# Second cross attention of a small perceiver: probabilities turned on VectorE in 32x32 blocks, values of two heads in one product with a ones column

## The chip, the cores and the metric

The kernel runs on one core of one Trainium2 chip. The metric is the device time of one execution in microseconds (us), the median of several. A profile is of one such execution; its times are counted from the first instruction of the span.

## What is computed

Six layers work on x, 64 sequences of 32 tokens with 256 features: a windowed cross attention, an attention, an fp8 feed-forward layer, a second cross attention (the one that is changed), a gated mixing layer and a mixture of experts. Each adds its output to x. The second cross attention, cut to its core:

```python
q = split(layernorm(x) @ w_q + b_q)            # 64 x 16 heads x 32 x 16
k = split(ctx_1024 @ w_k + b_k)                # 64 x 16 heads x 257 x 16
v = split(ctx_1024 @ w_v + b_v)
s = (q @ k.T) * 16 ** -0.5                     # 32 x 257 per head, masked
o = merge(softmax(s) @ v) @ w_o + b_o
x = x + o
```

All of it is float32, and 257 keys are one more than two blocks of 128 and one more than eight blocks of 32.

## The kernel before, in words

x lies in SBUF as 16 tiles `t` of 128 rows; a tile holds 4 sequences `b`. The stage of the second cross attention is `x1_tensor`, `x1_scalar`, `x1_vector` and `x1_pool`, one program for each engine, which meet through counting semaphores. Each goes over 16 tiles and the 4 sequences in each: 64 rounds. TensorE's program is written out for all tiles; the others loop.

Partitions carry (4 strips `j`) x (32 queries), and a round has 4 score groups `rg`, so 16 heads are 4 strips x 4 groups. One round of TensorE before is, in its order:

1. `scores` (L890): 8 products, weights of 32x64 (the spread queries), 257 moving columns, into PSUM banks 2 to 5.
2. second half of `values` of the round before (L918): weights are 32 columns of turned probabilities, moving data 16 columns of values, output in bank 7.
3. pieces `k0` and `k1` of the next sequence (L827): keys from the context, each product as three fp32r products of high and low parts (`exact`). `x1_piece` and `PIECES` write out the order; the pieces alternate between banks 0 and 1, and each needs its bank emptied (`kv0_free`, `kv1_free`).
4. `turn(t, b, 0)` (L903): 4 transposes of probabilities into bank 6.
5. piece `v` of the next sequence (L827), 12 products, 512 columns of one bank.
6. `turn(t, b, 1)` (L903), then the first half of `values` (L918).

In round b = 0 of a tile there is also the 257th key of the tile before: its probabilities are turned (piece `plT`, L865) and multiplied with values of that key made ahead of the stage (`x1_last_values`, `last_rows`, `last_key`, L929). In round b = 1 there is the piece `out` (L869), the output product of the tile before.

VectorE in a round: 4 reductions L1020 (mask, running minimum, `x1_nmax`), the two key copies L1005, the two copies of turned probabilities L1051; once a tile the reciprocals of the sums (L1026 to L1029), the scaling L1035, the block transpose of the heads L1054, the addition to x L1044 and its statistics L1058. ScalarE: 4 exponentials L987 with the sum accumulated, the value copy L972, the split of the next context and the mask. GpSimd: the low part of the context (L1076), the spread queries (L1085), a bias.

## Time and profile before

| | us |
|---|---|
| median of 3 runs | 1004.77 (1001.87 to 1009.84) |
| the profiled execution | 999.8 |
| its span | 998.0 |
| TensorE busy, share of the span | 91% |
| VectorE busy | 68% |
| ScalarE busy | 47% |
| GpSimd busy | 38% |

The span runs from the first to the last instruction of the profiled execution. Busy shares are averages over stages with different limits.

### The profile page before, as it was taken

The numbers are of one execution on the slowest core, as the hardware profiler recorded it, in microseconds if no ns is written. First come the engines' busy times: TensorE is split into PE (matmuls) and PEld (weight loads), VectorE is DVE, ScalarE is ACT, GpSimd is POOL, SyncE is SP. The second block draws the span as 40 slices with busy tenths as digits, with TensorE's granted clock in tenths as the row PEclk, the third lists the DMA queues.
The fourth block names the chain that finished last, engine by engine and source line by source line (L and its number), as shares of the span: only waits on it lengthen the run. The fifth ranks groups of instructions, "written<-read, shape, count | busy, mean of one in ns | idle before, by whom it ended". The sixth has DMA issues, their size and how long they took to land.

```text
span 998.0 us, 39451 instructions
## 1 busy us (share of the span) xinstructions
PE 906.3 (91%) x16050; PEld 741.3 (74%) x16050; DVE 680.4 (68%) x1765; ACT 465.8 (47%) x1197; POOL 381.5 (38%) x602
## 2 busy tenths in 40 slices
PE   4999889989746889999999999999977898999998
PEld 3777777777523678888888888888745568999976
DVE  5888798878775466666666666667568486555536
ACT  1222223322464645555555555556454434555541
POOL 6222223322396162333332242224047305766640
PEclk9999999999767999999999999999879799999999
DMA  7001400000001011111111111110037101222216
GB/s 254 25 19 56 155 4 4 5 4 4 3 1 48 3 50 51 51 50 54 62 66 65 52 50 51 50 50 3 2 132 307 43 0 59 81 75 77 79 65 237
DMA packets 29904, 60.96 MB, mean 61 GB/s; under 512 B 6000, under 2 KB 22480, under 8 KB 26416
## 3 DMA queue, kind: packets, MB, share of 16 engines
q1 hardware_dynamic: 25136, 48.00, 13.6%
q0 software_dynamic: 3744, 10.23, 3.0%
q8 instruction: 130, 2.13, 0.8%
q10 hardware_dynamic: 864, 0.36, 0.2%
q14 instruction: 30, 0.25, 0.1%
HBM read 49.27 MB, written 9.31 MB: 59 GB/s over the span
## 4 chain that ended last, share of the span: by engine, by line
PE 74%; issue 8%; DVE 7%; ACT 4%; POOL 4%; DMA 1%; DVEq 0%; ACTq 0%; POOLq 0%
PE psum L827 18%; PE psum L1605 7%; PE psum L903 7%; PE psum L261 6%; PE psum L234 4%; PE psum L890 3%; PE psum L1468 3%; PE psum L300 3%; PE psum L291 3%; PE psum L918 3%; PE psum L276 3%; ACT x_p L987 2%; PE psum L742 2%; PE psum L869 2%; PE psum L1488 1%
## 5 line engine op out<-in xcount | busy, mean ns | idle before, releaser
L987 ACT ACTIVATE x_p<-x_s,x_nmax 128x257 f32<-128x257 f32 x256 | 127.4, 500 | 100.0 <-DVE x_nmax L1020 99.9
L1051 DVE COPY x_pT<-psum 128x512 f32<-128x512 f32 x128 | 88.2, 689 | 56.3 <-PE psum L903 54.5
L1020 DVE CUSTOM_DVE_ANT_0 x_s<-psum,x_mask 128x257 f32<-128x257 f32 x256 | 94.3, 423 | 41.8 <-PE psum L890 41.1
L1076 POOL TENSOR_TENSOR x_ctx1l<-x_ctx,x_ctx1h 128x2064 fp32r<-128x2064 f32 x8 | 36.8, 4599 | 145.6 <-ACT x_ctx1h L770 145.6
L903 PE MATMUL psum<-ident,x_p 128*128 128x128 f32 x512 | 80.6, 280 | 5.6 <-ACT x_p L987 1.8
L1076 POOL TENSOR_TENSOR x_ctx0l<-x_ctx,x_ctx0h 128x2064 fp32r<-128x2064 f32 x7 | 32.2, 4599 | 104.1 <-ACT x_ctx0h L770 104.1
L903 PEld LDWEIGHTS psum<-ident,x_p 128*128 128x128 f32 x512 | 58.3, 141 | 17.1 <-ACT x_p L987 15.5
L918 PEld LDWEIGHTS psum<-x_v,x_pT 128*32 128x32 f32 x4096 | 48.3, 113 | 30.1 <-DVE x_pT L1051 18.2
L1708 POOL DMA_INDIRECT moe_outs<-me_out,me_goal x39 | 55.1, 1414 | 40.1 <-DVE me_out L1677 40.1
L1005 DVE TENSOR_SCALAR x_k<-psum,x_bk 128x258 f32<-128x258 f32 x128 | 57.7, 481 | 16.1 <-PE psum L827 16.1
L918 PE MATMUL psum<-x_v,x_pT 128*32 128x16 f32 x4096 | 61.0, 186 | 0.0
L972 ACT ACTIVATE x_v<-psum 128x512 f32<-128x512 f32 x64 | 38.2, 597 | 44.0 <-PE psum L827 44.0
L1699 POOL DMA_INDIRECT me_in<-moe_rows,me_token x39 | 39.7, 1018 | 45.3 <-DVE me_token L1454 33.7
L1677 DVE TENSOR_TENSOR me_out<-psum,me_eb 128x256 f32<-128x256 f32 x39 | 16.6, 425 | 58.0 <-PE psum L827 58.0
L325 ACT ACTIVATE sm_xT<-psum 128x256 f32<-128x256 f32 x32 | 12.3, 384 | 90.5 <-PE psum L224 90.5
L234 PE MATMUL psum<-sm_v,sm_pT 32*32 32x17 f32 x4096 | 42.6, 180 | 9.9 <-issue 6.8
L234 PEld LDWEIGHTS psum<-sm_v,sm_pT 32*32 32x32 f32 x4096 | 38.4, 104 | 17.3 <-issue 13.1
L827 PE MATMUL psum<-me_w2h,me_hTh 128*128 x156 | 47.2, 303 | 1.7 <-DVE me_hTl L1680 1.7
L987 ACT ACTIVATION_READ_ACCUMULATOR x_p<-x_s,x_nmax 128x1 f32 x256 | 47.8, 187 | 0.0
L1632 ACT ACTIVATE me_in<-psum 128x256 f32<-128x256 f32 x39 | 15.0, 385 | 67.8 <-PE psum L1592 67.8
L1645 ACT ACTIVATE me_out<-psum,me_eb 128x128 f32<-128x128 f32 x156 | 44.4, 374 | 1.3 <-PE psum L1605 1.3
L890 PE MATMUL psum<-x_k,x_qs 32*64 32x257 f32 x1024 | 44.6, 404 | 0.0
(293 smaller groups left out, 2744.3 us busy)
## 6 DMA issues: line engine op xcount, KB each, us to landing
x_ctx<-in_ctx SPq DMA_DIRECT2D x16, 1032.0 KB, 4.8
me_w<-in_moe_w SPq DMA_DIRECT2D x8, 1024.0 KB, 11.7
me_got<-moe_outs SPq DMA_DIRECT2D x8, 512.0 KB, 7.5
x_mask<-in_mask SPq DMA_DIRECT2D x16, 128.5 KB, 3.8
x<-in_x SPq DMA_DIRECT2D x4, 512.0 KB, 8.0
sm_cT<-in_ctx SPq DMA_DIRECT2D x16, 128.0 KB, 2.2
moe_rows<-me_xw SPq DMA_DIRECT2D x4, 512.0 KB, 4.9
me_ws<-in_moe_ws SPq DMA_DIRECT2D x1, 1024.0 KB, 4.8
```

What stands on the lines that cost most here:

```text
L234: mm = nc.tensor.matmul(psum[strip(b), O, h * DO:(h + 1) * DO], sm_pT[strip(b), u, h * S:(h + 1) * S], sm_v[strip(b), u, h, :], start=True ...
L261: nc.tensor.matmul(psum[:, QK + t % 2, s * D:(s + 1) * D], (kv if s else sm_xT)[:, u, k, :], c.w_qkv[:, k, s * D:(s + 1) * D], start=(s + ...
L827: mm = nc.tensor.matmul(out, v, w, start=(first and n == 0), stop=(last and n == len(pairs) - 1), **kw)
L890: mm = nc.tensor.matmul(psum[2 * S * m:2 * S * (m + 1), 2 + rg, 0:SK], x1_qs[rows, par, m, b, :], x1_k[rows, b % 2, m, 0:SK], start=True, ...
L903: mm = nc.tensor.transpose(psum[:, 6, (2 * r + k) * P:(2 * r + k + 1) * P], x1_p[:, column(b, CB * c + r), k * P:(k + 1) * P], ident[:])
L918: mm = nc.tensor.matmul(psum[S * j:S * (j + 1), 7, n * DH:(n + 1) * DH], x1_pT[:, c, r, k, j * S:(j + 1) * S], x1_v[:, b % 2, k, (j * G + ...
L987: nc.scalar.activation(x1_p[:, n, :], x1_s[:, rg, :], ACT.Exp, bias=x1_nmax[:, par, n:n + 1], scale=-1.0, accum_out=x1_sum[:, par, n:n + 1 ...
L1005: nc.vector.tensor_scalar(x1_k[:, b % 2, m, :], kv_bank(n)[:, 0:SP], x1_bk[:, m:m + 1], None, ALU.add).then_inc(x1[f"kv{n % 2}_free"], 1)
L1020: nc.vector.tensor_tensor_reduce(out=x1_s[:, rg, :], in0=psum[:, 2 + rg, 0:SK], in1=x1_mask[par][:, b, :], scale=1.0, scalar=-2 * MASKED, ...
L1051: nc.vector.tensor_copy(x1_pT[:, c].rearrange("p r k s -> p (r k s)"), psum[:, 6, :]).then_inc(x1["pT_ready"], 1)
L1076: eng.tensor_tensor(low[:], x1_ctx[:], high[:].bitcast(F32), ALU.subtract).then_inc(x1["ctx_split"], 1)
L1605: mm = nc.tensor.matmul(psum[:, i % 2, m * P:(m + 1) * P], me_up[i % 2][:, k * HID + m * P:k * HID + (m + 1) * P], me_sT[:, i % 2, k, :], ...
```

## The change

- The probabilities are no longer turned by TensorE into PSUM and copied. VectorE turns them in 32x32 blocks, from `x1_p` straight to `x1_pT`, 576 elements a partition and half (`turn` in `x1_vector`). `x1_p` has 288 columns: 257 of keys, one of `void` (the old `x1_void`, not a number where everything is masked) and zeros.
- `values` contracts 32 keys at a time. Weights are a block of turned probabilities of two heads, 32 rows x 64 columns; moving data are the values of both heads and a column of ones, 33 columns. Four strips `j` lie in four row groups of the array, strips 0 and 2 in its first 64 columns, 1 and 3 in its last; they write banks 6 and 7. Keys 257 and 258 (`void`) are a ninth block of 2 rows. That is 2 halves x 9 blocks x 4 strips = 72 products a round, in one go, between the key pieces and the value pieces.
- Of each 64x33 output, each head's rows need only their own 16 columns and the sum. `row_pick` is now 128x2 and selects them: VectorE forms reciprocals, multiplies them by `row_pick` and scales both banks with it (`x1_o2`); GpSimd adds the two halves (`x1_heads`).
- The values are made turned, features on partitions, as two pieces `v0` and `v1` with the same shape as the keys, and VectorE turns them in blocks into `x1_v`. The key copies go to ScalarE, whose own value copy goes. ScalarE's exponentials no longer accumulate.
- The output piece `out` becomes `o0` and `o1` of 128 columns each.
- The products, copies, splits, the load and the arrays of the 257th key alone go (`x1_last_values`, `x1_last_scalar`, `last_rows`, `last_key`, `plT`).
- The first value pieces are made after the last query products, and not before them.

The diff without most of the removed lines, which stand in the kernel above:

```diff
@@ -778,12 +744,14 @@
-        PIECES = [("plT", 0, -1), ("k0", 1, 0), ("k1", 1, 0), ("v", 1, 0),
-                  ("k0", 2, 0), ("k1", 2, 0), ("v", 2, 0), ("out", 0, -1),
-                  ("k0", 3, 0), ("k1", 3, 0), ("v", 3, 0),
-                  ("k0", 0, 1), ("k1", 0, 1), ("v", 0, 1)]
-        LEAD = 11
+        PIECES = [("k0", 1, 0), ("k1", 1, 0), ("v0", 1, 0), ("v1", 1, 0),
+                  ("k0", 2, 0), ("k1", 2, 0), ("v0", 2, 0), ("v1", 2, 0), ("o0", 0, -1), ("o1", 0, -1),
+                  ("k0", 3, 0), ("k1", 3, 0), ("v0", 3, 0), ("v1", 3, 0),
+                  ("k0", 0, 1), ("k1", 0, 1), ("v0", 0, 1), ("v1", 0, 1)]
+        LEAD = 14
         CB = BT // 2
+        KB = SK // S + 1
+        VO = 2 * DH + 1
         def column(b, rg):
...
@@ -832,44 +800,33 @@
         def x1_first_pieces(pe):
             pe.wait_ge(x1["w_split"], 4)
...
+            for k in range(2):
                 pe.sem_inc(x1[f"kv{k}_free"], 1)
...
+            for n in (LEAD, LEAD + 1):
                 x1_piece(pe, n, -1, 1, True)
         def x1_piece(pe, n, t, par, there):
             kind, b, whose = PIECES[n]
             kv_free(pe, n, t)
...
+            if not there:
                 pe.sem_inc(x1[f"kv{n % 2}_done"], 1)
                 pe.sem_inc(x1[f"kv{n % 2}_free"], 1)
                 return
...
             out = kv_bank(n)
+            m = slice(int(kind[1]) * P, int(kind[1]) * P + P)
             if kind == "k0" and b == 0:
                 pe.wait_ge(x1["ctx_split"], t + 1 + 1)
...
+            if kind[0] in "kv":
+                ct = x1_cs[(par + 1) % 2 if whose == 1 else par]
                 for k in range(KC):
...
+                    mm = exact(out[:, 0:SP], parts([w[:, k, m] for w in (x1_wks if kind[0] == "k" else x1_wvs)],
+                                                   [c[:, k, b * SP:(b + 1) * SP] for c in ct]), k == 0, k == KC - 1)
+            else:
+                pe.wait_ge(x1["oT_ready"], t)
                 for k in range(KC):
...
+                    mm = nc.tensor.matmul(out[:, 0:P], x1_oT[:, k * P:(k + 1) * P], x1_wo[:, k, m],
                                           start=(k == 0), stop=(k == KC - 1))
             mm.then_inc(x1[f"kv{n % 2}_done"], 1)
...
+            def values(t, b):
+                i = BT * t + b
+                for m in range(KC):
+                    kv_taken(pe, place(f"v{m}", b), t - (b == 0))
+                if i == 0:
+                    pe.wait_ge(x1["ones_ready"], 2)
+                if b == 0 and t > 0:
+                    pe.wait_ge(x1["heads_ready"], 2 * t)
+                for c in range(2):
+                    pe.wait_ge(x1["pT_ready"], 2 * i + c + 1)
+                    for kb in range(KB):
                         for j in range(L):
...
+                            rows = slice(S * j, S * j + (S if kb < KB - 1 else 2))
+                            e = c * BT + b
+                            mm = nc.tensor.matmul(psum[2 * S * (j % 2):2 * S * (j % 2 + 1), 6 + j // 2, e * VO:(e + 1) * VO],
+                                                  x1_pT[rows, b % 2, c, kb, :], x1_v[rows, b % 2, c, kb, :],
+                                                  start=(b + c + kb == 0), stop=False, skip_group_check=True)
                 mm.then_inc(x1["pv_done"], 1)
             def tile(t, par, before, own, after):
                 for b in range(BT):
+                    here = own if b < BT - 1 else after
                     if own:
                         scores(t, par, b)
...
+                    for n in (place("k0", (b + 1) % BT), place("k1", (b + 1) % BT)):
+                        piece(n, t, par, here)
+                    if b > 0 and own or b == 0 and before:
+                        values(t - (b == 0), (b - 1) % BT)
+                    for n in (place("v0", (b + 1) % BT), place("v1", (b + 1) % BT)):
+                        piece(n, t, par, here)
                     if b == 1:
...
+                        piece(place("o0"), t, par, before)
+                        piece(place("o1"), t, par, before)
+            for n in (LEAD + 2, LEAD + 3):
+                piece(n, -1, 1, True)
...
@@ -966,46 +896,57 @@
         def x1_scalar(act):
             nc.scalar.preload_act_table(ACT.Exp)
...
+            def take_keys(b, t, m):
+                n = place(f"k{m}", b)
                 kv_done(act, n, t)
...
+                nc.scalar.activation(x1_k[:, b % 2, m, :], kv_bank(n)[:, 0:SP], ACT.Identity,
+                                     bias=x1_bk[:, m:m + 1]).then_inc(x1[f"kv{n % 2}_free"], 1)
+            for m in range(KC):
+                take_keys(0, -1, m)
             def tile(t, par, before, own, after):
                 for b in range(BT):
...
+                    for m in range(KC):
+                        if own:
+                            for rg in range(CB * m, CB * (m + 1)):
+                                n = column(b, rg)
+                                act.wait_ge(x1["max_ready"], J * t + G * b + rg + 1)
+                                nc.scalar.activation(x1_p[:, n, 0:SK], x1_s[:, rg, :], ACT.Exp, bias=x1_nmax[:, par, n:n + 1],
+                                                     scale=-1.0).then_inc(x1["exp_ready"], 1)
+                        if own if b < BT - 1 else after:
+                            take_keys((b + 1) % BT, t, m)
                     if not after and own and b == 2:
                         mix_normalise(act, 0)
                     if after and b in (0, 1):
                         context_high(act, t + 1, 1 - par, b)
                     if after and b == 2:
                         mask(act, t + 1, 1 - par)
...
             x1_tiles(act, tile)
         def x1_vector(dve):
...
+            def take_values(b, t, i):
+                if not (isinstance(i, int) and i < 2):
+                    dve.wait_ge(x1["pv_done"], i - 1)
                 for m in range(KC):
...
+                    n = place(f"v{m}", b)
                     kv_done(dve, n, t)
...
+                    nc.vector.transpose(x1_v[:, b % 2, m, :, 0:2 * DH], kv_bank(n)[:, 0:KB * S]).then_inc(x1[f"kv{n % 2}_free"], 1)
+            def turn(t, b, c):
+                i = BT * t + b
+                n = column(b, CB * c)
+                hold(dve, x1["exp_ready"], J * t + G * b + CB * (c + 1))
+                if c == 0:
+                    dve.wait_ge(x1["void_ready"], i + 1)
+                if not (isinstance(i, int) and i < 2):
+                    dve.wait_ge(x1["pv_done"], i - 1)
+                nc.vector.transpose(x1_pT[:, b % 2, c].rearrange("p k (r q) -> p r k q", r=CB),
+                                    x1_p[:, n:n + CB, :].rearrange("p r (k s) -> p r k s", s=S)).then_inc(x1["pT_ready"], 1)
+            nc.vector.memset(x1_v[:, :, :, :, 2 * DH:VO].rearrange("p b c k o -> p (b c k o)"), 1.0).then_inc(x1["ones_ready"], 1)
+            take_values(0, -1, 0)
             def tile(t, par, before, own, after):
...
                             nc.vector.tensor_tensor_reduce(out=x1_s[:, rg, :], in0=psum[:, 2 + rg, 0:SK], in1=x1_mask[par][:, b, :], scale=1.0,
                                                            scalar=-2 * MASKED, op0=ALU.add, op1=ALU.min,
                                                            accum_out=x1_nmax[:, par, n:n + 1]).then_inc(x1["max_ready"], 1)
+                        dve.wait_ge(x1["max_ready"], J * t + G * (b + 1))
+                        if isinstance(t, int) and t + b == 0:
+                            dve.wait_ge(x1["ends_ready"], 1)
+                        own_columns = lambda v: v.rearrange("p (c b r) -> p c b r", c=2, b=BT)[:, :, b, :]
+                        nc.vector.tensor_scalar(own_columns(x1_p[:, :, SK]), own_columns(x1_nmax[:, par, :]), 1e10, 0.0, ALU.mult,
+                                                ALU.mult).then_inc(x1["void_ready"], 1)
+                    if b == 1 and before:
+                        dve.wait_ge(x1["o_ready"], t)
+                        nc.vector.transpose(x1_oT[:], x1_o[:]).then_inc(x1["oT_ready"], 1)
+                    if own:
+                        turn(t, b, 0)
                     if b == 0 and before:
...
+                        dve.wait_ge(x1["pv_done"], BT * t)
+                        both = psum[:, 6:8, 0:2 * BT * VO].rearrange("p j (n e) -> p j n e", e=VO)
+                        nc.vector.reciprocal(x1_rinv[:].rearrange("p (j n) -> p j n", j=2), both[:, :, :, 2 * DH]).then_inc(x1["rinv_ready"], 1)
                         dve.wait_ge(x1["rinv_ready"], 2 * t - 1)
...
+                        nc.vector.tensor_tensor(x1_pick[:], x1_rinv[:].unsqueeze(2).broadcast_to([P, 2 * 2 * BT, 2]),
+                                                row_pick[:].unsqueeze(1).broadcast_to([P, 2 * 2 * BT, 2]), ALU.mult).then_inc(x1["rinv_ready"], 1)
+                        dve.wait_ge(x1["rinv_ready"], 2 * t)
+                        if not (isinstance(t, int) and t == 1):
+                            dve.wait_ge(x1["o_ready"], t - 1)
+                        for j in range(2):
+                            own_pick = x1_pick[:, 2 * BT * j:2 * BT * (j + 1), :].unsqueeze(3).broadcast_to([P, 2 * BT, 2, DH])
+                            nc.vector.tensor_tensor(x1_o2[:, :, :, j * DH:(j + 1) * DH], both[:, j, :, 0:2 * DH].rearrange("p n (r d) -> p n r d", r=2),
+                                                    own_pick, ALU.mult).then_inc(x1["heads_ready"], 1)
+                    if own:
+                        turn(t, b, 1)
                     if own if b < BT - 1 else after:
...
+                        take_values((b + 1) % BT, t, BT * t + b + 1)
+                    if b == 1 and before:
+                        hold(dve, x1["x_biased"], t)
+                        for m in range(KC):
+                            n = place(f"o{m}")
                             kv_done(dve, n, t)
...
+                            row = x[:, bass.ds(t - 1, 1), m * P:(m + 1) * P].rearrange("p o c -> p (o c)")
+                            nc.vector.tensor_tensor(row, kv_bank(n)[:, 0:P], row, ALU.add).then_inc(x1[f"kv{n % 2}_free"], 1)
                     if b == BT - 1 and before:
...
+                        for m in range(KC):
+                            n = place(f"o{m}")
+                            hold(dve, x1[f"kv{n % 2}_free"], kv_count(n, t) + 1)
                         nc.vector.bn_stats(bn_out[:, bass.ds(t - 1, 1), :].rearrange("p o c -> p (o c)"),
                                            x[:, bass.ds(t - 1, 1), :].rearrange("p o c -> p (o c)")).then_inc(x1["stats_ready"], 1)
...
+        def x1_heads(pool, t):
+            pool.wait_ge(x1["heads_ready"], 2 * t)
+            if not (isinstance(t, int) and t == 1):
+                pool.wait_ge(x1["oT_ready"], t - 1)
+            nc.gpsimd.tensor_tensor(x1_o[:].rearrange("p (n c) -> p n c", c=2 * DH), x1_o2[:, :, 0, :], x1_o2[:, :, 1, :],
+                                    ALU.add).then_inc(x1["o_ready"], 1)
         def x1_pool(pool):
             pool.wait_ge(x1["bias_ready"], 1)
             pool.wait_ge(x1["norm_ready"], NT)
             pool.wait_ge(x1["q_ready"], KC * NT // U)
...
-            x1_last_values(pe)
...
+            act.wait_ge(x1["pT_ready"], 2 * BT * NT)
```

## Rows read from the trace of the kernel before

**Rows 1.** The page: busy us of each engine, share of the span, instructions.

```profile
PE 906.3 (91%) x16050; PEld 741.3 (74%) x16050; DVE 680.4 (68%) x1765; ACT 465.8 (47%) x1197; POOL 381.5 (38%) x602
```

**Rows 2.** Busy time by window of one tile; columns: engines, clock, DMA.

```profile
406.00:430.00 24.00, 23.79 (x462) 19.91 (x462) 16.50 (x58) 13.84 (x41) 6.72 (x6) 1.00 0.16 53
```

**Rows 3.** Timeline of TensorE's products over one tile: start, duration, engine, line.

```profile
504.58 0.69 PE L890 MATMUL psum<-x_k,x_qs 32*64 32x257 f32 x16
...
510.84 0.69 PE L890 MATMUL psum<-x_k,x_qs 32*64 32x257 f32 x16
...
517.29 0.69 PE L890 MATMUL psum<-x_k,x_qs 32*64 32x257 f32 x16
...
522.87 0.69 PE L890 MATMUL psum<-x_k,x_qs 32*64 32x257 f32 x16
523.49 0.45 PE L918 MATMUL psum<-x_v,x_pT 128*32 128x16 f32 x32
...
525.65 0.66 PE L903 MATMUL psum<-ident,x_p 128*128 128x128 f32 x4
...
527.55 0.60 PE L903 MATMUL psum<-ident,x_p 128*128 128x128 f32 x4
528.08 0.45 PE L918 MATMUL psum<-x_v,x_pT 128*32 128x16 f32 x32
528.45 0.69 PE L890 MATMUL psum<-x_k,x_qs 32*64 32x257 f32 x16
```

**Rows 4.** The chain that ended last, in the stage: start, us, what.

```profile
514.27 1.42 PE psum L827 x12
```

**Rows 5.** Timeline of TensorE's weight loads in three other places of the kernel.

```profile
154.41 1.16 PEld L234 LDWEIGHTS psum<-sm_v,sm_pT 32*32 32x32 f32 x128 [0.17 <-issue]
...
759.10 1.86 PEld L1350 LDWEIGHTS psum<-me_rw,me_xT 128*128 128x128 f32 x16
760.88 1.60 PEld L1231 LDWEIGHTS psum<-mx_wo,mx_glob 96*128 96x128 f32 x8
```

**Rows 6.** The group of products with 8 moving columns: busy us, mean ns.

```profile
L1350 PE MATMUL psum<-me_rw,me_xT 128*128 128x8 f32 x64 | 8.5, 268 | 2.3 <-ACT me_xT L1363 2.3
```

**Rows 7.** VectorE's groups by form: busy us, mean ns, idle before.

```profile
L1020 DVE CUSTOM_DVE_ANT_0 x_s<-psum,x_mask 128x257 f32<-128x257 f32 x256 | 94.3, 423 | 41.8 <-PE psum L890 41.1 <-issue 0.5
...
L441 DVE STREAM_TRANSPOSE sm_pT<-sm_p 128x512 f32<-128x512 f32 x32 | 22.5, 702 | 1.4 <-ACT sm_p L344 1.4
...
L1054 DVE STREAM_TRANSPOSE x_oT<-x_o 128x256 f32<-128x256 f32 x16 | 7.0, 435 | 0.0
L1035 DVE TENSOR_TENSOR x_o<-psum,x_rinv 128x256 f32<-128x256 f32 x16 | 6.6, 415 | 3.1 <-PE psum L929 3.1
```

**Rows 8.** Timeline of VectorE: the first reductions of two rounds.

```profile
518.44 0.43 DVE L1020 CUSTOM_DVE_ANT_0 x_s<-psum,x_mask 128x257 f32<-128x257 f32 x1 [0.58 <-PE psum L890]
...
518.79 0.42 DVE L1020 CUSTOM_DVE_ANT_0 x_s<-psum,x_mask 128x257 f32<-128x257 f32 x1
```

**Rows 9.** ScalarE's groups by form.

```profile
L987 ACT ACTIVATE x_p<-x_s,x_nmax 128x257 f32<-128x257 f32 x256 | 127.4, 500 | 100.0 <-DVE x_nmax L1020 99.9
...
L1256 ACT ACTIVATE mx_y<-psum,mx_conv 128x256 f32<-128x256 f32 x16 | 6.8, 481 | 0.0
```

**Rows 10.** Timeline of the stage's start.

```profile
333.06 0.69 PE L890 MATMUL psum<-x_k,x_qs 32*64 32x257 f32 x16
...
333.87 1.28 ACT L967 ACT_TABLE_LOAD   x1
...
340.11 0.69 PE L890 MATMUL psum<-x_k,x_qs 32*64 32x257 f32 x16
```

**Rows 11.** Timeline of the stage's end: last scores, last addition to x.

```profile
713.74 0.69 PE L890 MATMUL psum<-x_k,x_qs 32*64 32x257 f32 x16
...
727.15 0.42 DVE L1044 TENSOR_TENSOR x<-psum,x 128x256 f32<-128x256 f32 x1 [2.37 <-PE psum L869]
```

**Rows 12.** Waits of TensorE in 20 to 262 us: total, times, longest.

```profile
PEld psum L234 <- issue: 13.1, 40, 1.9
```

More of the change, by code:

```diff
@@ L39 @@
 L = BT
-LAST = 32
 KC = D // P
@@ L2022, in layout @@
     pairs = np.concatenate([ctx, ctx[..., 2 * SK - SP:SK]], axis=-1)
-    order = [b for _ in range(2) for b in range(BT) for _ in range(2)]
-    last = ctx[..., SK - 1][..., order * (LAST // len(order))]
     out["ctx"] = pairs.reshape(NT, P, KC, BT * SP)
-    out["xattn1_cl"] = last.transpose(1, 2, 0, 3).reshape(P, KC, NT * LAST)
     out["ctx32"] = np.ascontiguousarray(
@@ L2098, in layout @@
     out["causal"] = np.where(np.arange(S)[None] > (p % S)[:, None], CAUSAL, 0.0).astype(np.float32)
[L2099 to L2100 removed]
+    out["row_pick"] = (p[:, None] // S % 2 == np.arange(2)[None]).astype(np.float32)
     out["half_scale"] = (((p[:, None] // DH) % 2 == np.arange(2)[None]) * -DH ** -0.5).astype(np.float32)
```

204 lines of the change are left out of this document (20 added, 184 removed).

## The prediction

> **What bounds the kernel now.** I read the busy line first: TensorE works 91% of the span, VectorE 68% [rows 1]. A share over the whole span hides the stages, so next the window of one tile inside the changed stage: TensorE busy 23.79 of 24.00 us, VectorE 16.50, ScalarE 13.84, clock 1.00, which is the 2.4 GHz level [rows 2]. The stage is TensorE's program laid end to end; another engine matters only where it makes TensorE wait. So the timeline of one tile gives the terms. Score products start at 504.58, 510.84, 517.29, 522.87 and 528.45 [rows 3]: rounds of 6.26 (257th key), 6.45 (output product), 5.58 and 5.58, a tile of 23.87. The plain round from 522.87 divides into scores 0.62 (to 523.49); values, two key pieces and a wait 2.16 (to 525.65); a turn and the value piece 1.90 (to 527.55); the second turn 0.53; values 0.37. The value piece is 12 products in 1.42 [rows 4], so one is 0.12, the key pieces 1.44, the first turn 0.48, and what is left of the 2.16, 0.35, is the wait for the exponentials.
>
> **What leaves TensorE's round.** Two turns, 0.48 + 0.53; the wait, 0.35, because nothing on TensorE waits for this round's probabilities any more; values, 2 x 0.37. Together 2.10.
>
> **What comes.** 72 products of 32x64 weights and 33 moving columns. Each float32 product is two records (8 score products are x16 in the rows), so 144 loads and 144 streams. Four strips run side by side, so they come in 36 waves of four. What does a wave cost? By the moving columns next to nothing. But look at products whose streams are short. With 128x128 float32 weights and 8 moving columns [rows 6], 16 loads take from 759.10 to 760.88, 0.111 us each [rows 5]: that is the load, since eight columns are no work. With 32-column weights, 128 loads take 1.16 in all, 9.1 ns each at most; less the last one's own length, which I put at 0.10, 8.3 ns, and a wave of four 33 ns [rows 5]. The load's time goes by the columns of the weights. For 64 columns I take the point on the line between the two: 33 + (111 - 33) / 3 = 59 ns. 36 waves are 2.12 us; the drain behind them I take from the old values, 0.37 less 8 waves of 33 ns, 0.11. Together 2.23.
> The trace has no such wave. From below, loads might cost what 32 columns cost: 36 x 33 ns + 0.11 = 1.30. From above, two strips share 64 columns of the array and might load in turn: 36 x 118 ns + 0.11 = 4.36. Against the upper end speak the scores, four row groups of which share each half: in 0.62 us no row of loads in turn fits beside two streams of 257 columns. I stay with 2.23.
> The Trainium skill ("TensorE: Matmul & The Clock Gate", LDWEIGHTS) says that a load takes its columns over 1.2 in ns, whatever the rows. The trace agrees roughly, 111 ns for 128 columns where it gives 107 [rows 5]. By it a wave is 53 ns and the values 2.03 instead of 2.23.
> The array goes from whole to tiled and back: before, one such entry stands behind the second turn, 0.05 (0.53 against 0.48) to 0.17 (the idle time ahead of the small attention's burst [rows 5]); now there are two, ahead of the values and of the scores. I take 0.13 each, 0.26. The value pieces are 258 columns wide instead of 256: 0.02.
> So a plain round goes from 5.58 to 5.58 - 2.10 + 2.23 + 0.26 + 0.02 = 5.99. It is longer by 0.41: the blocks of 32 keys need 144 loads of 64 columns where there were 64 loads of 32 and 8 transposes.
>
> **The two special rounds.** Round 0 loses its surplus, 6.26 - 5.58 = 0.68 (`plT`, L929). Round 1 keeps 0.87: the two halves of the output product stream as many columns.
>
> **Does VectorE hold it up?** Reductions come every 0.35 (518.44, 518.79), the first some 1.16 after the scores start (517.29) [rows 3, 8]. Block transposes: 512 elements 0.70, 256 elements 0.435 [rows 7], so 1.04 ns an element; 576 are 0.77, 288 about 0.47, from PSUM taken alike (bounds 0.4 and twice that). A round holds 4 x 0.35 + 0.25 (`void` and waits) + 2 x 0.70 + 2 x 0.40 with overlap = 3.85 of 5.99. Turned halves are ready at 3.5 and 4.5 after the scores' start and are wanted in the next round. `v0` is made at about 5.1 and `v1` at 5.85, taken by 5.6 and 6.5; the next keys want the first bank at 6.6 and the second at 7.3. ScalarE has 4 exponentials of under 0.50 and 2 key copies of 0.48 with a bias [rows 9]: 2.9, and at most 1.05 more for context or mask. Covered. If transposes took double, `v1` would be taken at 8.1 and the round would grow by 0.5.
> In round 0 VectorE stops between its turns for `pv_done` of the tile before (4.4 after the scores), then a reciprocal, a small product and two scalings of 0.415 [rows 7], with the waits some 1.3, and its second turn and both takings queue behind. `v0` is free at about 6.8 where TensorE wants it at 6.6: 0.2. In round 1 the output halves follow the value pieces at once and wait for both takings: `o0` 0.1, `o1` 0.3. GpSimd's addition ahead of its context split is needed a round later, and GpSimd works 6.72 of 24.00 us [rows 2].
> Tile: 4 x 0.41 - 0.68 + 0.6 = +1.56; over 15.5 tiles +24.2 us.
>
> **Start, end, rest.** Scores began at 333.06 because VectorE had copied the first keys long before. Now ScalarE copies them, after its table load ends at 335.15 [rows 10]; `v0` and `v1` want these banks, so the first scores start near 337.0. The old first round was long, 7.05 (to 340.11); the new one has no values but waits for exponentials and key copies in turn, 5.3: the second scores start at 342.3, +2.2. At the end 13.4 lie between the last scores and the last addition (713.74 to 727.15) [rows 11]; `plT` and L929 go, a GpSimd addition and two scalings come: -1. The products of the 257th key ahead of the stage (24 records of 0.12, beside waiting queues): 0 to -3, I take -0.5.
> Then code. The small attention asks for some 444 loads and products in 6.9 us, 64 per us, and waits for issue before its bursts, 13.1 us in 40 times, the longest 1.9 [rows 12]; part of it is the array's change. The new round asks for 61 per us, with 288 in a burst of 2.2 us, against 40 before. 0 to 15 us; I take 4.
> Sum: 24.2 + 2.2 - 1 - 0.5 + 4 = +28.9. The profiled execution took 999.8, so the same execution would take 1028.7. The median of the runs lies 5 above it; 1004.8 + 28.9 = 1033.7, I say 1033.
>
> **Rivals.**
> - The loads don't bound: a wave costs what 32 columns cost, 33 ns. Values 1.30, round 5.06, tile 4 x (-0.52) - 0.68 + 0.6 = -2.16, over the stage -33.5; with start and end +0.7 and 4 for code -29: 976. For it: turns, copies and the wait do go, and all tiles load beside each other. Against: [rows 5] twice, at two widths. The point from which it decides is a wave of 47 ns or less (then the tile is even). Chance 0.14.
> The Trainium skill ("TensorEngine Tiling (Array Packing)", Instruction Overhead) has a rule that leads there: a matmul has some 60 cycles of overhead, so that one free column costs as much as 60. By that alone a wave is 25 ns, less than in this rival.
> - In between: waves near 50 ns and few stalls; within 1% of before. Chance 0.08.
> - VectorE becomes the bound: transposes out of `x_p` or PSUM, in patterns of four dimensions, take double. Then each round is 0.5 longer, +31 on the forecast: 1064. Against: L1054 and L441 show about one element per cycle. Chance 0.07.
> - Row groups with common columns load in turn: values 4.36, +2.1 a round, 1165. Chance 0.03.
> - That the change doesn't do what it says, here: TensorE still waits for this round's probabilities. The order of `tile` excludes it but for VectorE's delay, which is above.
> - The forecast, 1033, between 1018 (waves of 53 ns, no code waits) and 1050: 0.68.
>
> **How the numbers follow.** A measurement of this kernel tells about 1% from no change. Faster 0.14, within 1% 0.08, slower 0.78. The range leaves out the first and the fourth rival, 0.17: 996 to 1062.
>
> **What would show it.** Score starts 6.0 apart in plain rounds, against 5.58; the 144 records of values over 2.2 us, loads of one strip 59 ns apart; no wait of TensorE for exponentials; VectorE idle before the value takings; a tile of some 25.4 us. It would be wrong if the loads of a strip were 35 ns apart, or if TensorE's idle time before key pieces grew over 0.5 a round.

## The result and the profile after

The changed kernel takes 1063.37 us (median of 4 runs, 1057.65 to 1068.68) against 1003.32 (median of 4, 994.90 to 1009.84: the three runs of the table of before and one more): 1.060 of the time before, with an interval of 1.055 to 1.066. It is slower by 60 us. The forecast was 1033, also slower, but by half as much, and 1063 lies just outside the range.

The page of the profiled execution (1068.68 us, span 1066.9): the busy line, as [rows 1], and the line of the queue that brings instructions (packets, MB, share).

```profile
PE 956.9 (90%) x20538; PEld 798.3 (75%) x20538; DVE 714.2 (67%) x1847; ACT 444.1 (42%) x986; POOL 378.4 (35%) x602
...
q8 instruction: 164, 2.69, 1.0%
```

TensorE has 4,488 more products and works 51 us longer; ScalarE and GpSimd work less. Before, the instruction queue had 130 packets.

TensorE in one plain round, which answers to 522.87 to 528.45 of [rows 3]: products and weight loads, the start, the duration, the engine.

```profile
530.23 0.69 PE L847 MATMUL psum<-x_k,x_qs 32*64 32x257 f32 x16
...
530.85 0.19 PEld L795 LDWEIGHTS psum<-x_ctx1h,x_wkh 128*128 128x128 f32 x1 [0.39 <-issue]
...
532.48 2.19 PEld L865 LDWEIGHTS psum<-x_v,x_pT 32*64 32x64 f32 x144
534.71 0.19 PEld L795 LDWEIGHTS psum<-x_ctx1h,x_wvh 128*128 128x128 f32 x1
...
536.36 0.47 PE L847 MATMUL psum<-x_k,x_qs 32*64 32x257 f32 x8
```

The 144 loads take 2.19 us, and the value pieces start 2.23 us after the first of them: the forecast's figure. The key pieces with their entry take 1.63 (530.85 to 532.48) and the value pieces 1.65, of which 1.44 each is the work. The round is 6.13 long.

VectorE's and ScalarE's groups by form, to compare with [rows 7, 9].

```profile
L945 DVE STREAM_TRANSPOSE x_pT<-x_p 128x576 f32<-128x576 f32 x128 | 98.6, 772 | 10.4 <-ACT x_p L915 2.4
...
L935 DVE STREAM_TRANSPOSE x_v<-psum 128x288 f32<-128x288 f32 x128 | 59.4, 473 | 93.4 <-PE psum L795 93.4
...
L915 ACT ACTIVATE x_p<-x_s,x_nmax 128x257 f32<-128x257 f32 x256 | 115.9, 502 | 235.6 <-DVE x_nmax L961 235.6
L902 ACT ACTIVATE x_k<-psum,x_bk 128x258 f32<-128x258 f32 x128 | 58.5, 458 | 1.3 <-PE psum L795 1.2
```

The transposes take 0.77 and 0.47 us, as worked out. VectorE stands idle 93.4 us ahead of the value takings: it waits for TensorE there, not the reverse.

Where the extra time lies shows in the starts of the score products (L890 before, L847 after; 64 in either). They are the marks of the rounds. In the profiled pair, 68.9 us apart:

| stretch | before | after | more | forecast |
|---|---|---|---|---|
| up to the last query product | 332.54 | 339.76 | 7.2 | -0.5 |
| from there to the second scores | 7.57 | 10.54 | 3.0 | 2.2 |
| second to last scores (15.5 tiles) | 373.63 | 426.76 | 53.1 | 24.2 and most of 4 |
| last scores to the mixer's first product | 15.8 | 19.5 | 3.7 | -1 |
| the rest | | | 1.9 | 0 |

The first line is not the change's. Another execution with the code of before up to there (e9 below) had its last query product at 339.49. Without it the sum is 61.7, and the medians are 60.1 apart.

In the stage, undisturbed rounds take 6.11, 7.66, 6.12 and 6.12, a tile of 26.02 against 23.88. 15.5 such tiles are 403 us, 33 more than before. The stage took 426.8. Before, its tiles lay 3.5 us in all above their usual length; now it is 23.4. So 20 of the 53 us are not in the round as it is written. (The 3.5 of before lie in one tile: a wait of 2.82 us for VectorE's key copy at 363.49, and a lower clock behind it.) Two rows of the waits of TensorE, 345 to 765 us (total, times, longest):

```profile
PE psum L865 <- issue: 5.8, 11, 1.5
...
PEld psum L795 <- DVE x_v L935: 9.4, 15, 0.7
```

The second is what the forecast had, one wait a tile for the bank behind VectorE's late taking in round 0; this column also holds time in which earlier products still run, and TensorE's own idle share of it is about 0.2 us a tile. The first is new. TensorE stops inside a burst of value products, and no engine is what it waits for. The timeline of its weight loads at the longest such place in the middle of the stage:

```profile
420.18 0.19 PEld L795 LDWEIGHTS psum<-x_ctx1h,x_wkl 128*128 128x128 f32 x1 [0.71 <-issue]
420.49 1.95 PEld L865 LDWEIGHTS psum<-x_v,x_pT 32*64 32x64 f32 x127
424.02 0.61 PEld L865 LDWEIGHTS psum<-x_v,x_pT 32*64 32x64 f32 x17 [1.58 <-issue]
...
427.57 0.33 PEld L847 LDWEIGHTS psum<-x_k,x_qs 32*64 32x64 f32 x16 [0.23 <-issue]
```

127 loads, a stop of 1.58, and the last 17 take 0.61 instead of 0.26. The clock is lower here, too. Windows (length, busy us of the engines, clock, DMA share, GB/s) over this place, over an undisturbed tile, and over a like place later:

```profile
416.00:428.00 12.00, 10.03 (x204) 8.66 (x212) 4.97 (x15) 2.76 (x7) 0.00 (x0) 0.78 0.20 74
...
482.00:509.00 27.00, 26.41 (x748) 23.16 (x747) 18.80 (x61) 12.59 (x27) 7.46 (x7) 1.00 0.14 48
609.00:621.00 12.00, 10.04 (x203) 8.58 (x201) 4.96 (x16) 2.54 (x6) 0.00 (x0) 0.72 0.10 35
```

How firmly the clock hangs on the stops is answered below the table of the experiments. Read here also what a tile asks for: 748 products and 747 loads in 27.00 us, 55 instructions per us, where [rows 2] have 38.5. Most of the experiments turn on this figure.

### The profile page after: what moved, and what is told of

The parts are those of the page before. It is cut to its first block, busy times and chain, and to the rows that moved or that the text cites. A ratio compares the mean times of both kernels' runs of the same rounds, so it can differ in the third digit from the quotient of the medians.

```text
span 1066.9 us, 48206 instructions
## 1 busy us (share of the span) xinstructions
PE 956.9 (90%) x20538; PEld 798.3 (75%) x20538; DVE 714.2 (67%) x1847; ACT 444.1 (42%) x986; POOL 378.4 (35%) x602
## 4 chain that ended last, share of the span: by engine, by line
PE 77%; issue 8%; DVE 7%; POOL 4%; ACT 3%; DMA 1%; DVEq 0%; PEldq 0%; ACTq 0%; POOLq 0%
PE psum L795 22%; PE psum L865 13%; PE psum L1549 7%; PE psum L260 6%; PE psum L233 4%; PE psum L847 3%; PE psum L1412 3%; PE psum L299 3%; PE psum L290 3%; PE psum L275 2%; PE psum L827 2%; PE psum L708 1%; PE psum L1432 1%; PE psum L246 1%; PE psum L1294 1%
## 5 line engine op out<-in xcount | busy, mean ns | idle before, releaser
L865 PE MATMUL psum<-x_v,x_pT 32*64 32x33 f32 x9216 | 155.6, 221 | 8.3 <-issue 7.9
L865 PEld LDWEIGHTS psum<-x_v,x_pT 32*64 32x64 f32 x9216 | 146.9, 136 | 19.1 <-issue 9.7
L935 DVE STREAM_TRANSPOSE x_v<-psum 128x288 f32<-128x288 f32 x128 | 59.4, 473 | 93.4 <-PE psum L795 93.4
L945 DVE STREAM_TRANSPOSE x_pT<-x_p 128x576 f32<-128x576 f32 x128 | 98.6, 772 | 10.4 <-ACT x_p L915 2.4
L1041 POOL TENSOR_TENSOR x_o<-x_o 128x256 f32<-128x256 f32 x16 | 11.6, 728 | 246.5 <-DVE x_o L987 246.5
L902 ACT ACTIVATE x_k<-psum,x_bk 128x258 f32<-128x258 f32 x128 | 58.5, 458 | 1.3 <-PE psum L795 1.2
L847 PE MATMUL psum<-x_k,x_qs 32*64 32x257 f32 x1024 | 46.4, 414 | 1.8 <-PEq L813 1.1
L487 POOL TENSOR_TENSOR x<-x,attn_b_o 128x256 f32<-128x256 f32 x16 | 12.2, 762 | 90.9 <-ACT sm_xn L317 90.9
L795 PE MATMUL psum<-me_w2l,me_hTh 128*128 x156 | 44.0, 282 | 0.0
L795 PE MATMUL psum<-me_w2h,me_hTl 128*128 x156 | 43.9, 281 | 0.0
L795 PE MATMUL psum<-x_ctx0h,x_wvh 128*128 128x258 f32 x128 | 40.3, 315 | 3.9 <-ACT x_k L902 2.8
```

The costliest lines, as they stand in the source:

```text
L795: mm = nc.tensor.matmul(out, v, w, start=(first and n == 0), stop=(last and n == len(pairs) - 1), **kw)
L847: mm = nc.tensor.matmul(psum[2 * S * m:2 * S * (m + 1), 2 + rg, 0:SK], x1_qs[rows, par, m, b, :], x1_k[rows, b % 2, m, 0:SK], start=True, ...
L865: mm = nc.tensor.matmul(psum[2 * S * (j % 2):2 * S * (j % 2 + 1), 6 + j // 2, e * VO:(e + 1) * VO], x1_pT[rows, b % 2, c, kb, :], x1_v[row ...
L902: nc.scalar.activation(x1_k[:, b % 2, m, :], kv_bank(n)[:, 0:SP], ACT.Identity, bias=x1_bk[:, m:m + 1]).then_inc(x1[f"kv{n % 2}_free"], 1)
L935: nc.vector.transpose(x1_v[:, b % 2, m, :, 0:2 * DH], kv_bank(n)[:, 0:KB * S]).then_inc(x1[f"kv{n % 2}_free"], 1)
L945: nc.vector.transpose(x1_pT[:, b % 2, c].rearrange("p k (r q) -> p r k q", r=CB), x1_p[:, n:n + CB, :].rearrange("p r (k s) -> p r k s", s ...
```

## The experiments

A record here is one product or load of TensorE as the trace has it. Times are medians; the kernel before ran on the same chip beside each. "Idle on issue" is TensorE's idle time of over 0.3 us between the second and the last scores that nothing in the profile ends: 9.8 us in 13 places in the changed kernel, 0 before.

**e1, e2: weight columns against moving columns.** Of each value product half of the weight columns (e1) or about half of the moving columns (e2) are left out.

```diff
-psum[2 * S * (j % 2):2 * S * (j % 2 + 1), ...], x1_pT[rows, b % 2, c, kb, :], ...
+psum[2 * S * (j % 2):2 * S * (j % 2) + S, ...], x1_pT[rows, b % 2, c, kb, 0:S], ...      # e1
-... e * VO:(e + 1) * VO], ..., x1_v[rows, b % 2, c, kb, :],
+... e * VO:e * VO + DH + 1], ..., x1_v[rows, b % 2, c, kb, 0:DH + 1],                    # e2
```

> Theory A (the loads bound the values, and a load goes by the columns of its weights): 32 of the 64 weight columns leave a wave of 33 ns in place of 59, a burst of 144 records takes 1.3 us in place of 2.3, plain rounds near 5.2 us in place of 6.1, and the run loses 50 to 60 us: near 1008. Rival B (the streams or the number of products bound): waves stay at 59 ns and the time at 1063. The second head of each pair is left out of the products.

> Theory A (the loads bound): 17 moving columns in place of 33 change nothing: waves of 59 ns, 1063 within 8 us. Rival B (the streams bound): waves of some 33 ns and a run near 1008. The second head's values and the ones column are left out of the products.

e1: 1035.36 (1025.02 to 1042.90), ratio 1.026 (1.015 to 1.036). e2: 1068.58 (1065.63 to 1072.42), ratio 1.065 (1.057 to 1.073). 17 moving columns take as long as 33. The weight columns count: the timeline of e1 has the same 144 loads in 1.31 us, 36 ns a wave against 2.19 and 61.

```profile
541.26 1.31 PEld L865 LDWEIGHTS psum<-x_v,x_pT 32*32 32x32 f32 x144
```

But the time fell by some 30 us only (28 by the medians, 31 without the longest of e1's runs), where the loads were worth 55. The waits of e1 say where the other half went (345 to 765 us; 27.1 of the 29.9 lie before the last scores at 750.4):

```profile
PE psum L865 <- issue: 29.9, 28, 2.8
```

Idle on issue grew from 9.8 to 35.6 us. Rounds of 5.3 us occur, the shortest tile is 21.94, yet the mean tile is 26.2.

**e3, e9: the context's load.** Every tile loads 1 MB of context in about 5 us, and several stops come right behind it. Both kernels were run with an eighth of it; the products then use stale context.

```diff
-sp.dma_start(x1_ctx[:], a["ctx"][t])
+sp.dma_start(x1_ctx[:, :, 0:SP // 2], a["ctx"][t][:, :, 0:SP // 2])
```

> Theory C (TensorE's idle stretches inside bursts of values are late code, held up by the context load, and each also brings a stretch at the low clock): with an eighth of the context loaded per tile the stage loses most of its idle time put down to issue, some 11 us, and its stretches at half clock; plain rounds stay at 6.1 us; the run takes 1040 to 1053. Rival D (they come from TensorE's own code or from waits, whatever the loads): 1063 within 8 us, with as many idle stretches. Seven eighths of the context stay that of the first tile.

> The kernel before with an eighth of each context loaded per tile (the rest of the work is the same; the products then use stale context), as the changed kernel had in its own run with the small context (1050 against 1063). Theory A (the stalls that this load brings are the changed kernel's: only a burst of 288 instructions leaves TensorE without instructions when its 16 KB transfers run beside the load): within 1% of before, 0 to -4 us, and the stage at 370 to 373 us. Theory B (the load costs either kernel the same): 988 to 993.

e3, the changed kernel: 1050.34 (1048.57 to 1053.11), ratio 1.048 (1.040 to 1.056), 13 us less. e9, the kernel before: 1003.81 against 1005.61, ratio 0.997 (0.993 to 1.000), nothing that can be told. The load costs only the changed kernel. In e3 idle on issue is 2.2 us, and the stage is 12 us shorter with the same undisturbed rounds.

**e4, e12: by place or by chance?** e4 puts 128 waits in place of one ahead of the stage on TensorE; the trace has 63 more instructions of TensorE for it (657 semaphore instructions against 594 in e3), and all later instructions move by as many places. e12 is the changed kernel once more.

```diff
-            pe.wait_ge(f8["x_updated"], NT)
+            for _ in range(128):
+                pe.wait_ge(f8["x_updated"], NT)
```

> 128 more waits, all passed already, ahead of the stage on TensorE. Theory C: the places of the idle stretches move, since other instructions stand at the borders of what is fetched, and the time stays within 8 us of 1063. Rival D (a fixed instruction or wait makes each stretch): they stay at the same rounds.

> The changed kernel once more, unchanged, for one look. If the stalls of TensorE on issue in the stage belong to places of the code, most of the 13 seen (at 419.7, 422.6, 453.6, 610.7, 645.6, 779.9 and others, counted from the stage's start) come at the same round and the same product; if they go by chance, at others. Both expect 1057 to 1069 us.

e4: 1055.78 (1053.16 to 1061.88). e12: 1061.07, one run. e12 stops where the first execution did. Here is the place shown above, in e12:

```profile
415.94 0.19 PEld L795 LDWEIGHTS psum<-x_ctx1h,x_wkl 128*128 128x128 f32 x1 [0.87 <-issue]
416.25 1.95 PEld L865 LDWEIGHTS psum<-x_v,x_pT 32*64 32x64 f32 x127
419.51 0.60 PEld L865 LDWEIGHTS psum<-x_v,x_pT 32*64 32x64 f32 x17 [1.30 <-issue]
```

Again after 127 loads. The third and fourth tile take 30.00 and 28.68 in one execution, 29.89 and 28.93 in the other; the tenth and eleventh 30.95 and 28.99, and 29.55 and 28.76. In e4 the third and fourth take 27.32 and 27.00, and the long ones are the fifth (28.09), the twelfth (29.44) and the thirteenth (28.85). Idle on issue is 8.2 us there. So the stops belong to places in TensorE's instructions, and moving the code moves them without removing them.

The traces tell which places. TensorE's instructions come by a DMA queue of their own (the line q8 of the page), in packets of 256, as e5 shows below. Count TensorE's instructions in the order of the trace: loads, products, and those for semaphores and registers. All 13 stops on issue of the changed kernel's stage stand at a count with the same remainder by 256, and so do, each within its own trace, all 171 of the twelve traces that have any. And TensorE goes on 1.2 to 1.6 us after a packet has ended. The packet for the stop at 422.55 began at 421.41 and took 1.17 us; TensorE went on at 424.02. So a stop is the place where TensorE has used up, to the instruction, what had come. The 63 instructions of e4 moved these borders within the stage.

**e5: fewer waves.** Four of nine blocks of keys are left out of the value products.

```diff
-                    for kb in range(KB):
+                    for kb in range(0, KB, 2):
```

> Leaves out four of the nine blocks of keys in the value products (blocks 1, 3, 5 and 7), so each round issues 80 of 144 products, 20 waves for 36; columns and everything else stay. Theory A (what the 32-column run did not give back went to instructions that arrive late: a burst of 288 instructions in 2.1 us, or in 1.3 us with 32 columns, runs ahead of their transfers): here the burst is about as short as in the 32-column run (20 x 59 = 1.2 us) but has 160 instructions, so the idle stretches of TensorE put down to issue go below those of the changed kernel and the time falls by 62 x 0.94 = 58 and some 10 to 15 us of stalls: 985 to 1000. Theory B (something else, VectorE or ScalarE, ends the round once the burst is short): as the 32-column run, 1030 to 1040.

976.61 us (976.11 to 982.19), ratio 0.973 (0.967 to 0.980): 87 us less than the changed kernel, and below the kernel before. Undisturbed rounds are 5.18 instead of 6.12, 0.94 for 16 waves, 59 ns a wave: 58 us over the stage. The rest of the gain in the stage, some 21 us, are the stops and what follows them: there are none. The time lies below both forecasts. The window over one of its tiles, and the page's line of the instruction queue:

```profile
482.00:504.30 22.30, 22.01 (x488) 18.77 (x487) 18.46 (x60) 12.37 (x28) 10.76 (x20) 1.00 0.16 55
```

```profile
q8 instruction: 132, 2.16, 0.9%
```

The tile asks for 44 instructions per us. The whole kernel has 8,192 fewer, and 32 packets of instructions fewer: 256 to a packet of 16 KB. The Trainium skill ("Advanced Engine Details and Errata", ISA Cache) gives the same unit, a line of 16 KB for 256 instructions; it speaks of only two such lines and, beside that, of 128 KB on TensorE. The two packet counts agree with the unit. For two lines speaks that, counted from the places where TensorE stops, no trace here has a packet that ended further ahead of it than 562 instructions.

**e6: the burst cut in two.** The products of the second half of the heads run behind the piece `v0`.

```diff
+                    for c in range(2):
+                        values(..., c)
+                        piece(place(f"v{c}", (b + 1) % BT), t, par, here)
```

> Same work; the value products of the first half of the heads run ahead of the piece v0, those of the second half between v0 and v1, so no run of short instructions is longer than 144 in a row. Theory A (late instructions cost the stage about 20 us because 288 of them come in one burst): fewer and shorter stalls, less the switches between tile shapes, 62 more at about 0.13 us (+8): 1045 to 1060. Theory B (the stalls go by the number of instructions and the transfers beside them, not by their order): stalls as before and the switches come on top: 1065 to 1075.

1087.26 us (1075.90 to 1089.00), ratio 1.080 (1.071 to 1.088): worse by 24. Plain rounds are 6.44, 0.32 more for one more change of the tile's shape and back. The round with the output pieces is 8.4, for it waits longer for the bank behind VectorE's taking (13.5 us in 15 times, by the waits of products). Stops on issue are fewer (5.4 us in 5 places), but tiles lie 18 us in all above 28.03, and the time is above both forecasts. Halving the burst does not take the cost of late instructions away.

**e7, e8, e11: three repairs.** e7 has VectorE copy the first two keys and puts all four first pieces ahead of the last query products. e8 puts the output pieces ahead of the value pieces in round 1. e11 is e7 with the context loaded in two halves, the second 11 us later.

```diff
+            for m in range(KC):                                                   # e7, in x1_vector
+                nc.vector.tensor_scalar(x1_k[:, 0, m, :], kv_bank(n)[:, 0:SP], x1_bk[:, m:m + 1], None, ALU.add)
...
-                    for n in (place("v0", ...), place("v1", ...)): piece(...)     # e8
                     if b == 1: piece(place("o0"), ...); piece(place("o1"), ...)
+                    for n in (place("v0", ...), place("v1", ...)): piece(...)
...
-                sp.dma_start(x1_ctx[:], a["ctx"][t])                              # e11
+                sp.dma_start(x1_ctx[:, 0, :], a["ctx"][t][:, 0, :])
+                hold(sp, x1["scores_done"], BT * (t - 1) + 1)
+                sp.dma_start(x1_ctx[:, 1, :], a["ctx"][t][:, 1, :])
```

> The first two keys' banks are copied by VectorE (not ScalarE, which first loads the table of the exponential), and all four first pieces stand ahead of the last queries as two do now. Theory A (the first scores wait for ScalarE's table load and copies): first scores about 4 us sooner after the last query product, 1057 to 1061. Theory B (the start is late only because the unchanged part ahead of it is): 1062 to 1066.

> In the second round of a tile the two output pieces come ahead of the two value pieces, and VectorE adds them before it turns the values. Theory A (the second round, 7.67 us against 6.12 of a plain one, holds 0.3 to 0.5 us of waiting for a bank behind VectorE's turn of the values, beyond the output products' own 1.0 to 1.2 us): 1055 to 1060. Theory B (the wait only moves to the value pieces): 1061 to 1067.

> The changed kernel with the start of the stage by VectorE (first keys' copies there, first pieces together) and each context loaded in two halves of 516 KB, the second one 11 us behind the first. Theory A (stalls need several us of a busy queue beside a late instruction transfer): half of the load's 13 us come back on top of the start's 4: 1048 to 1056. Theory B (two short loads catch as many instruction transfers as one long): 1056 to 1062.

e7: 1057.31 (1055.74 to 1061.79). The start of the changed kernel, then that of e7:

```profile
341.09 1.28 ACT L897 ACT_TABLE_LOAD   x1
...
342.39 0.84 ACT L902 ACTIVATE x_k<-psum,x_bk 128x258 f32<-128x258 f32 x2
...
344.90 1.16 PE L847 MATMUL psum<-x_k,x_qs 32*64 32x257 f32 x16
...
350.30 0.69 PE L847 MATMUL psum<-x_k,x_qs 32*64 32x257 f32 x16
```

```profile
330.35 0.69 PE L847 MATMUL psum<-x_k,x_qs 32*64 32x257 f32 x16
...
331.16 1.28 ACT L894 ACT_TABLE_LOAD   x1
...
335.86 0.69 PE L847 MATMUL psum<-x_k,x_qs 32*64 32x257 f32 x16
```

From the last query product (339.76 and 329.83) to the second scores it is 10.5 us and 6.0: 4.5 gained. The gain in the trace is sure; the medians differ by 6, within their spread. e8: 1061.32 (1055.40 to 1071.42). Without the longest run its median is 1058.02, so the time fits either theory. The trace speaks for B: round 1 falls from 7.66 to 7.59 only, since the value pieces now wait behind VectorE's additions (0.24 at 519.10). e11: 1054.95 (1053.02 to 1064.60), ratio 1.050 (1.043 to 1.057). It is the fastest that still does all of the work, with idle on issue at 8.3 us; how much of its 8 us is from the halves can't be told from the start's 4.5.

**e10, e13, e14: burst or total?** e10 is e1 with the small context. e13 is e1 with e5's five blocks, e14 is e1 with seven blocks (`kb in (0, 1, 2, 3, 4, 5, KB - 1)`).

> The 32-column run (half of the weight columns of each value product, the second head left out) with an eighth of each context loaded. Theory A (36 us of idle there go by the rate at which one burst of 1.3 us takes 288 instructions, whatever else is moved): 1020 to 1036, idle on issue in the stage still above 20 us. Theory B (late instructions need the context's transfers beside them): 985 to 1005, idle below 8 us.

> Leaves out the second head (32 of 64 weight columns) and blocks 1, 3, 5 and 7 of the value products: 80 of 144 products a round, each burst as fast as in the 32-column run (36 ns a wave, 0.73 us), but only 240 records a round, some 49 per us. Theory rate (instructions come late when a tile wants more than the supply of about 60 per us): no stalls on issue in the stage, rounds of 4.7 and 6.3, 940 to 955. Theory burst (the speed of the burst itself counts): stalls of some 10 us or more as with 32 columns and all blocks, 960 to 975.

> As before but seven of nine blocks: 112 products a round in a burst of 1.0 us, 304 records a round of 5.0 us without stalls, 57 per us over a tile, what the changed kernel wants. Theory rate: few stalls, as in the changed kernel, 2 to 12 us in the stage: 962 to 978. Theory burst: 15 to 30 us of stalls, nearer to those of 32 columns with all blocks: 980 to 995.

e10: 1020.78 (1015.48 to 1024.94), ratio 1.015 (1.009 to 1.021). 26 us of idle on issue remain with hardly any transfer beside: the load makes it worse (12 to 15 us here, 13 in e3) and is not needed for it. e13: 964.58 (961.13 to 969.82), ratio 0.960 (0.954 to 0.966). e14: 986.31 (985.25 to 989.37), ratio 0.980 (0.976 to 0.984). First e13's window over a tile, then e14's waits in the stage:

```profile
482.00:504.00 22.00, 21.33 (x491) 17.51 (x492) 18.55 (x60) 12.60 (x27) 11.07 (x21) 1.00 0.17 57
```

```profile
PE psum L865 <- issue: 10.9, 7, 2.1
```

e13 has bursts as fast as e1's and not one stop. e14 has 12.1 us of them in 8 places: at the edge of what the theory of the rate allowed (2 to 12), while its time lies in the bracket of the other theory (980 to 995). Side by side, where "wanted" is the records of a tile by its undisturbed length, and "above" is what the stage takes over 15.5 such tiles (e1's tile is its shortest, and e10's is taken from e1):

| kernel | records a tile | tile | wanted per us | above, us | idle on issue | half clock, us |
|---|---|---|---|---|---|---|
| before | 924 | 23.88 | 39 | 3.5 | 0 | 3.4 |
| e5, 5 blocks | 976 | 22.3 | 44 | 1.7 | 0 | 0 |
| e13, 5 blocks, 32 columns | 976 | 21.38 | 46 | 2.1 | 0 | 0 |
| e6, burst in two | 1488 | 28.03 | 53 | 18 | 5.4 | 23.9 |
| e3, small context | 1488 | 26.02 | 57 | 11 | 2.2 | 6.8 |
| after | 1488 | 26.02 | 57 | 23.4 | 9.8 | 17.1 |
| e14, 7 blocks, 32 columns | 1232 | 21.64 | 57 | 23 | 12.1 | 17.1 |
| e10, 32 columns, small context | 1488 | 21.94 | 68 | 46 | 26.2 | 0 |
| e1, 32 columns | 1488 | 21.94 | 68 | 66 | 35.6 | 23.9 |

The last column is the time between the second and the last scores in which the trace has TensorE's granted clock at 0.5, the 1.2 GHz level.

With the context's full load, the excess goes by the instructions wanted per us over a tile, and hardly by the speed within a burst: e13 has the fastest bursts and no stop. Two kernels that want 57, with bursts of 2.2 and 1.0 us, lose 5.8 and 6.9% of the stage; a small part of the burst in that is not excluded. The half clock is a second cost, and it does not follow the stops alone. In the changed kernel 6.8 us of it begin at 422.7, just into the stop of 1.47 us at 422.55, but none comes with the stop of 1.02 at 453.58. e10 has 26 us of stops, the longest 1.8, and not one stretch at half clock in the stage.

What e1 and e10 got is the mean supply where it is the limit: 1488 in 26.2 us, 57 per us, and 1488 in 24.9, 60 per us with an eighth of the context's load.

e13's time is nevertheless in the bracket of the other theory. The reason is a second bound. Its rounds are 5.00, not 4.7, and its waits, 345 to 670 us, name the copies out of the two banks:

```profile
PEld psum L795 <- DVE x_v L935: 16.9, 30, 0.8
PEld psum L795 <- ACT x_k L902: 13.8, 52, 0.4
```

e14 has the 5.00 that were forecast for it. Its time is over the bracket because it lies 23 us above its undisturbed tiles, where the bracket counted the stops alone.

## Why the prediction was half right

- **The price of a wave: right.** 59 ns, on a line between 32 and 128 columns, gave 2.23 us for the value products, and 2.23 was measured; e5 gives 59 ns a wave by difference. The rival in which the loads don't bound falls (they are 36 ns at 32 columns and 61 at 64, e1), and so does the one in which row groups load in turn.
- **The wait for the exponentials is gone**, the turns are gone, the transposes cost what was said, and VectorE does not hold up the plain round. The rival "VectorE becomes the bound" named 1064, the time that came; its mechanism is not what happened. VectorE waits for TensorE 93.4 us ahead of its takings, and in e5 it keeps up with rounds of 5.18.
- **The plain round: mis-sized by 0.13.** 6.12 against 5.99. The entries at the key and value pieces cost 0.19 and 0.21, not 0.13 each. e6 priced such a pair again, at 0.32. Over the stage this is 8 us.
- **The special rounds: about right.** Forecast 0.6 a tile of stalls; measured 0.26 at the start of round 1 and 0.43 for the output pieces in it. 1 us over the stage.
- **The code: this step failed.** "0 to 15 us; I take 4": late instructions and half clock cost the stage 20 us, and more at the end: 9.8 are stops, and the half clock takes 17.1 us against 3.4 before; an estimate from these two numbers is that the 13.7 more cost at most their half, 6.9. The ground for the 4 was a comparison of rates, 61 per us wanted against 64 in the small attention's bursts, and the step took the small attention's idle time as part array change. It was late packets almost alone: in the kernel before, 9.2 of the 10.2 us that TensorE idles there on issue, in waits of over 0.3 us (20 to 262 us), lie in ten stops at the borders of 256, and TensorE goes on 1.3 to 1.5 us after a packet. What it lacked was the comparison over a tile, not over a burst: the small attention's rate holds for 6.9 us, the new one for 430. It put no clock on the stops either.
- **Start: 3.0 against 2.2**, right in mechanism, and e7 takes it back.
- **End: wrong sign, 3.7 against -1.** One late packet is behind it. TensorE stops 2.04 us at 779.92 in the last value products, again at a border of 256, and the clock of the end is 0.59:

```profile
777.00:800.00 23.00, 15.21 (x326) 11.57 (x324) 10.03 (x28) 7.48 (x15) 5.39 (x9) 0.59 0.01 2
```

```profile
781.96 1.28 PE L865 MATMUL psum<-x_v,x_pT 32*64 32x33 f32 x36 [2.04 <-issue]
...
791.90 2.05 PE L827 MATMUL psum<-x_wo,x_oT 128*128 128x128 f32 x8 [2.76 <-DVE x_oT L972]
...
796.55 0.50 PEld L1150 LDWEIGHTS psum<-mx_xT,mx_w 128*128 128x128 f32 x2 [2.90 <-issue]
```

The two longer waits behind it are none of late packets: the first is for VectorE's turned heads, both stand at no border, and e5, which has no late packet, has them with 2.8 and 2.6 us too. In e4, whose borders lie elsewhere, there is no stop at the end, and it takes 14.2 us at a clock of 0.86. The kernel before took 15.8 at 0.59 in one execution and 12.6 at 0.88 in another (e9), so whether the step itself gains the forecast's 1 us is not shown.
- **The sum:** 28.9 forecast; 16 more for late instructions in the stage, 9 for the rounds as written, 5 for the end, 1 for the start make 60, what the medians show.

Open: why a packet is late at one border and not at the next. Packets of instructions come 4 to 5 us apart in the changed kernel's stage. The two longest gaps, 9.1 us (408.82 to 417.91) and 9.8 (600.46 to 610.23), come ahead of the stops at 419.67, 422.55 and 610.68, and each closes as a context's load ends (418.37 and 610.23). In the first of them TensorE began 438 instructions, where a packet has 256. With the small context or the load in halves no gap is over 7.2 us (e3 7.2, e11 6.9, e10 6.0). So the load goes with the longest ones, but whether it holds the packet back or only its request came late is not shown. Nor is what draws the half clock, and some 3 of the 20 us are neither in the 9.8 of stops nor in the 6.9 of the estimate. A value product in a number format with fewer passes, which would halve the instructions, was not tried.

## What to carry to other kernels

When a change trades few wide matrix instructions for many small ones, count the instructions of a whole tile and divide by the tile's new length, next to counting the array's time. In this kernel, beside a load of 1 MB a tile, up to 46 per us came free of stops, 53 to 57 cost 4 to 7% of the stage, and 68 could not be had. Then a saving in array time is partly given back (e1 kept some 30 of 55 us), while a saving in instructions pays twice (e5: 58 us of loads and some 21 us of stops and half clock). To tell such stops from other waits, count TensorE's instructions up to each: if the counts have one remainder by 256, they are late packets, and the kernel before shows them already. And a transfer that costs a kernel nothing can cost the next version 13 us, when the instructions come beside it.

## What was not expected of the hardware

- The supply of TensorE's instructions has a limit near 57 to 60 per us over long stretches; a tile that wants 57 loses time already, at borders of 256 instructions that repeat between executions and move when the code moves. Packets of 256 never began less than 3.2 us apart in any run.
- Around stops of 1.5 and 2.0 us the clock was lower, 0.78 over 12 us at 416 and 0.72 at 609, with 1.00 in an undisturbed tile; but 26 us of stops of up to 1.8 us (e10) went by without it.
- Loads of 32 rows in four strips side by side cost 36 ns a wave at 32 columns and 61 at 64, while 17 or 33 moving columns made no difference.
- An exponential of 257 columns took 502 ns without its running sum, against 500 with it [rows 9]; reading the sum took 187 ns more.
